# Flamingo-style gated block (selective scan, then a ternary feed-forward): where two one-value loads are issued, products of ones on TensorE in the front, and a new order of the written-out pieces

## The chip, the cores and the metric

One Trainium2 chip, one of its cores. The metric is the device time of one execution in microseconds, the median of three runs. All data is fp32 in HBM at the start and the result goes back there.

## The reference

The input `x` is (4, 256, 256): batch, tokens, channels; the context is (4, 256, 128). Two gated branches are added to `x`, one after the other.

```python
# branch 1: selective scan over the context, gated by silu(layernorm(x))
xi    = einsum('ed,bld->bel', in_proj_w, ctx)              # 256 channels
u     = silu(causal_conv4(xi) + conv_b)
x_dbl = einsum('ke,bel->bkl', x_proj_w, u)                 # 8 dt rows, 16 B rows, 16 C rows
delta = softplus(dt_proj_w @ dt_rows + dt_proj_b)
A     = -exp(A_log)                                        # (256, 16)
state = state * exp(delta*A) + (delta*u) * B_t             # for each of 256 tokens
y_t   = sum_n state[:, n] * C_t[n]
x     = x + tanh(g_xattn) * (y + D*u) * silu(layernorm(x))
# branch 2: per-token 8-bit activations, ternary weights
q     = round(layernorm(x) * 128/absmax)                   # w_gate, w_up: (1024, 256)
h     = silu(gate(q)) * up(q)
x     = x + tanh(g_ffn) * down(act_quant(walsh_hadamard(h)))   # w_down: (256, 1024)
```

The three weight matrices are scaled by the mean of their absolute values and rounded to -1, 0 or 1 inside the kernel.

## The kernel before, in words

The kernel is written by hand, with no scheduler at run time: each engine has a program that is a list of calls of small pieces, in an order written out, and each piece waits on semaphores for what it needs. An engine works through its list strictly in order. The four batches are the outer unit. In the scan the 16 states of a batch are taken two at a time, so there are 32 steps, m = 8 * batch + j. For step m and half h of the channels:

- `decays(m, h)` (ScalarE, L1036) writes exp(delta*A), two activations of 128x255.
- `drive_rows(m, h)` (TensorE, L397) multiplies the transposed delta*u by diagonal matrices of B, so that B*(delta*u) stands in PSUM.
- `scan(m, h)` (DVE, L1611) runs the recurrence over both.
- `C_rows(m)` (TensorE, L444) spreads C over the partitions, `times_C(m)` (DVE, L1694) multiplies, `accumulate(m)` (TensorE, L460) transposes the products into the sum over states.

POOL builds the diagonals (`diagonals(n, i)`, L1432) from the copy of B that `copy_BT(n)` (ScalarE, L1047) makes. It also takes the bf16 pieces of B and C apart (`split`), finishes softplus for later batches, scales weights and does the Walsh-Hadamard stages between 128-wide blocks (`fold_tile`).

The front, before the first scan, makes the first batch's u and delta. Loads come on two queues: SyncE (context, in_proj_w, x_proj_w, context, x, w_gate, w_up, w_down, hadamard; L312 to L323) and ScalarE (identity, conv_w, conv_b, dt_proj_w, the two gates, A_log, dt_proj_b, D; L962 to L973). The first batch's in_proj goes straight from the transposed weights; ScalarE makes the first tap (`first_tap`, L981) and DVE the others (`first_conv`, L1658), then `silu_u(0)` (L1069), `x_dbl(0)` (TensorE, L505), `dt_rows(0)` (L1103), `dt_proj(0)` (L523), `spread(0)` and `softplus(0)` on ScalarE, `first_relu`, `first_rest`, `first_delta` on DVE, `du_T(0)` (TensorE, L430) and `copy_duT(0)` (ScalarE, L1054). Beside it stand the transposes of the tap weights (`setup_in_proj`, L366, copied by `inw_out`) and of the other contexts (`setup_late`, L383, copied by `ctx_out`), which the later batches need, `in_proj(1, h)` (L489), `tanh_gates` (L999, waits for both gates and A_log), `exp_A` (L1004), `first_rstd` (layer norm of x, on ScalarE and DVE) and `weight_abs(m)` (ScalarE, L1023), the sum of absolute values of weight m. `for_silu` and `for_exp` load ScalarE's function table.

The wait that the loads feed is one semaphore for both of the last two:

```python
def spread(n):
    act.wait_ge(pe_draw, n + 1)
    if n == 0:
        act.wait_ge(ld_conv, 16 * 2)      # dtb and dskip
```

`dtb` is wanted by `spread(0)` and `first_relu`, `dskip` by `diag_D` (POOL, L1516) alone.

The tail, after the last scans, is the feed-forward of the last two tiles of tokens of batch 2 and of batch 3, in halves (`last_*`), with `hadamard_mm(2, 1)` (L610), `last_silu` (L1208), `last_fold` on DVE (L1797, L1800), `down(2, 1)` (L632) and `last_hadamard` (L684).

## Time and profile before

| what | value |
|---|---|
| median of 3 runs | 221.41 us (221.14 to 222.14) |
| the profiled execution | 220.58 us, span 218.8 us |
| DVE busy | 188.0 us, 86% |
| PE busy | 188.9 us, 86% |
| ScalarE (ACT) busy | 168.9 us, 77% |
| POOL busy | 108.0 us, 49% |
| mean granted TensorE clock | 0.966 |

The span is from the first to the last instruction; the execution's own time holds 1.78 us beside it. A granted clock of 1.00 is 2.4 GHz, 0.50 is 1.2 GHz. PE's busy time counts the time in flight of pipelined matmuls, so it overstates how full the engine is. In a timeline row, equal instructions that follow each other are merged and counted (x4); an fp32 product stands there as two records, an fp32 transpose as one.

### The profile page before, as it was taken

Reading aid. Unit: us, or ns where it says so; the run is one execution under the profiler, and the core shown is the slowest. Engines: PE = TensorE matmul, PEld = TensorE weight load, DVE = VectorE, ACT = ScalarE, POOL = GpSimd, SP = SyncE. Lnnn points to the kernel's source line nnn. Section 1 sums busy time; section 2 is a strip of 40 time slices with the busy share of each in tenths; the row PEclk is TensorE's granted clock in tenths of the full one; section 3 lists DMA queues with packets and bytes.
Section 4 is the critical chain, followed back from the end, with each engine's and each line's share of the span. In section 5 each row is a group of like instructions: output and inputs, shape, how many; then the busy total and the mean of one; then the engine's idle time right before and its main releaser. Section 6 shows DMA issues by size and latency. Waiting matters only on the chain. (4 is left out here: it accounts for less than half of the span.)

```text
span 218.8 us, 3665 instructions
## 1 busy us (share of the span) xinstructions
PE 188.9 (86%) x1221; PEld 152.7 (70%) x1228; DVE 188.0 (86%) x290; ACT 168.9 (77%) x298; POOL 108.0 (49%) x143
## 2 busy tenths in 40 slices
PE   2747889999899999899999999998998987686773
PEld 1534567887697998578989897797885776653751
DVE  1384938899999999998999999999989996889983
ACT  0278799999989969898967989993997811895373
POOL 1004700678708388029998991299920489510000
PEclk9965599999999999999999999999999999999998
DMA  5894000000000000000000000000000000000001
GB/s 135 264 343 182 0 1 4 0 0 0 3 0 0 3 1 1 0 3 0 1 3 0 0 3 24 1 27 0 0 0 3 25 0 27 0 0 0 27 24 48
DMA packets 8147, 6.33 MB, mean 29 GB/s; under 512 B 2202, under 2 KB 7874, under 8 KB 8130
## 3 DMA queue, kind: packets, MB, share of 16 engines
q1 hardware_dynamic: 6066, 6.01, 8.4%
q10 hardware_dynamic: 2064, 0.10, 0.6%
q8 instruction: 10, 0.16, 0.3%
q14 instruction: 7, 0.06, 0.1%
HBM read 5.05 MB, written 1.05 MB: 28 GB/s over the span
## 5 line engine op out<-in xcount | busy, mean ns | idle before, releaser
L1036 ACT ACTIVATE decay<-delta,zero_c,aneg 128x255 f32<-128x255 f32 x128 | 65.8, 588 | 1.6 <-DVE delta L1686 1.4
L1611 DVE TENSOR_TENSOR_SCAN state<-decay,BC 128x512 f32<-128x512 f32 x32 | 38.8, 1212 | 5.6 <-PE BC L397 3.8
L1611 DVE TENSOR_TENSOR_SCAN state<-decay,UP 128x512 f32<-128x512 f32 x32 | 38.4, 1201 | 1.1 <-issue 0.6
L1694 DVE TENSOR_TENSOR prod<-state,BC 128x1024 f32<-128x1024 f32 x32 | 38.4, 1200 | 0.7 <-PE BC L444 0.5
L1498 POOL TENSOR_TENSOR wnat<-wnat 128x512 f32<-128x512 f32 x18 | 22.9, 1275 | 26.2 <-DVE wnat L1738 25.4
L397 PE MATMUL BC<-diagB,duT 128*128 128x256 f32 x128 | 33.7, 386 | 0.7 <-DVE state L1611 0.5
L460 PE MATMUL PY<-id,prod 128*128 128x128 f32 x256 | 33.2, 273 | 1.1 <-DVE prod L1694 1.1
L397 PE MATMUL UP<-diagB,duT 128*128 128x256 f32 x128 | 33.3, 382 | 0.0
L460 PEld LDWEIGHTS PY<-id,prod 128*128 128x128 f32 x256 | 29.2, 141 | 3.9 <-DVE prod L1694 1.7
L397 PEld LDWEIGHTS BC<-diagB,duT 128*128 128x128 f32 x128 | 22.3, 190 | 5.2 <-issue 2.0
L397 PEld LDWEIGHTS UP<-diagB,duT 128*128 128x128 f32 x128 | 22.7, 190 | 3.6 <-issue 1.2
L1499 POOL TENSOR_TENSOR wnat<-wnat 128x512 f32<-128x512 f32 x18 | 22.9, 1274 | 0.0
L1432 POOL TENSOR_SCALAR_AFFINE_SELECT diagB<-BT 128x1024 f32<-128x1024 f32 x16 | 18.5, 1174 | 6.4 <-PE UP L397 4.4
L1163 ACT COPY hT<-GP 128x1024 f32<-128x1024 f32 x6 | 6.0, 1005 | 13.0 <-PE GP L594 13.0
L444 PE MATMUL BC<-bc,sel 96*128 96x256 bf16 x64 | 12.5, 276 | 1.0 <-DVE prod L1694 1.0
L1454 POOL TENSOR_TENSOR rest<-raw,high 64x256 f32<-64x256 f32 x4 | 2.7, 666 | 21.1 <-ACT raw L1098 21.1
L579 PE MATMUL GP<-wT,qT 128*128 128x512 bf16 x42 | 11.0, 379 | 1.9 <-DVE state L1611 0.9
L444 PEld LDWEIGHTS BC<-bc,sel 96*128 96x128 bf16 x64 | 6.1, 100 | 4.9 <-issue 2.3
L1159 ACT ACTIVATE wq<-GP,zero_c,gs 128x1024 f32<-128x1024 f32 x6 | 7.2, 1206 | 2.6 <-PE GP L579 2.6
L974 ACT ACT_TABLE_LOAD x1 | 1.3, 1283 | 9.4 <-issue 9.4
L579 PEld LDWEIGHTS GP<-wT,qT 128*128 128x128 bf16 x48 | 4.2, 97 | 5.8 <-ACT qT L1174 1.4
L610 PEld LDWEIGHTS GP<-had,hT 128*128 128x128 f32 x64 | 7.7, 192 | 0.8 <-ACT hT L1163 0.6
(250 smaller groups left out, 383.1 us busy)
## 6 DMA issues: line engine op xcount, KB each, us to landing
xs<-in_x_dram SPq DMA_DIRECT2D x1, 1024.0 KB, 8.8
wnat<-in_L_ffn_w_gate_dram SPq DMA_DIRECT2D x1, 1024.0 KB, 12.0
wnat<-in_L_ffn_w_up_dram SPq DMA_DIRECT2D x1, 1024.0 KB, 14.5
wnat<-in_L_ffn_w_down_dram SPq DMA_DIRECT2D x1, 1024.0 KB, 13.9
out_dram<-ot SPq DMA_DIRECT2D x8, 128.0 KB, 1.7
ctxs<-in_ctx_dram SPq DMA_DIRECT2D x1, 384.0 KB, 4.3
ctxs<-in_ctx_dram SPq DMA_DIRECT2D x1, 128.0 KB, 2.9
inw<-n_L_xattn_in_proj_w_dram SPq DMA_DIRECT2D x1, 128.0 KB, 2.6
```

What stands on the lines that cost most here:

```text
L397: last = nc.tensor.matmul(drive_bank(h).rearrange("p (n c l) -> p n c l", n=NB, c=LC)[:, :, c, :], duT[:, b % 2, c, P * h:P * (h + 1)], di ...
L444: last = nc.tensor.matmul(PC[:, L * n:L * (n + 1)], row_pick(DS + NB * j + n), bc3[:, b, :], start=True, stop=True)
L460: last = nc.tensor.matmul(PY[:, E * c + P * h:E * c + P * (h + 1)], prod[:, g % RING, h, n, P * c:P * (c + 1)], id32[:], is_transpose=True ...
L579: last = nc.tensor.matmul(ffn_bank(f, t)[:, 512 * i:512 * (i + 1)], qT[:, h, P * t:P * (t + 1)], w[:, h, 512 * i:512 * (i + 1)], start=(h ...
L610: last = nc.tensor.matmul(dst[:, P * a:P * (a + 1)], hT[:, t, a, :], had[:], start=True, stop=True)
L1036: last = nc.scalar.activation(decay[:, m % RING, h, n, 1:L], delta[:, b % 2, h, 1:L], ACT.Exp, bias=zero_c[:], scale=aneg[:, h, NB * j + n ...
L1159: nc.scalar.activation(sg[:, t], ffn_bank(f, t)[:], ACT.Silu, bias=zero_c[:], scale=gs[:, t:t + 1]).then_inc(act_sg, 1)
L1432: nc.gpsimd.affine_select(diagB[:, i].rearrange("p c n l -> p (c n) l"), BT[:, n % 2, i].rearrange("p c n -> p (c n)").unsqueeze(2).to_bro ...
L1498: nc.gpsimd.tensor_tensor(dst[:, :, 0, :], src[:, :, 0, :], src[:, :, 1, :], ALU.add)
L1499: nc.gpsimd.tensor_tensor(dst[:, :, 1, :], src[:, :, 0, :], src[:, :, 1, :], ALU.subtract).then_inc(done, 1)
L1611: nc.vector.tensor_tensor_scan(state[:, g % STATES, h].rearrange("p n l -> p (n l)"), decay[:, g % RING, h].rearrange("p n l -> p (n l)"), ...
L1694: nc.vector.tensor_tensor(prod[:, g % RING].rearrange("p h n l -> p h (n l)"), state[:, g % STATES].rearrange("p h n l -> p h (n l)"), PC. ...
```

## The change

Three things are changed.

The loads of dtb and dskip leave ScalarE's queue. dtb goes to SyncE's queue between x and w_gate, with a semaphore of its own (`ld_dtb`), dskip to its end behind hadamard (`ld_D`).

TensorE gets pieces that multiply a matrix of ones by itself, into PSUM that is overwritten later; no one reads them. There are 12 calls of `warm` and 5 of `warm_later`, two products each.

The order of the pieces is new in all four programs, over the whole kernel; the pieces themselves are as they were.

```diff
             sp.dma_start(xs[:].rearrange("p b c d -> p (b c) d"), tiles(x)).then_inc(ld_x, 16)
+            with nc.allow_non_contiguous_dma(reason="one value per partition"):
+                sp.dma_start(dtb[:], dt_proj_b.rearrange("(h p) -> p h", p=P)).then_inc(ld_dtb, 16)
...
             sp.dma_start(had[:], hadamard).then_inc(ld_had, 16)
+            with nc.allow_non_contiguous_dma(reason="one value per partition"):
+                sp.dma_start(dskip[:], D.rearrange("(h p) -> p h", p=P)).then_inc(ld_D, 16)
...
+            def warm(i):
+
+                if i == 0:
+                    pe.wait_ge(consts, 1)
+                for n in range(2):
+                    nc.tensor.matmul(X[:, P * n:P * (n + 1)], onesf[:], onesf[:], start=True, stop=True)
+
+            def warm_later(i):
+
+                pe.wait_ge(act_setup, 2)
+                for n in range(2):
+                    nc.tensor.matmul(PB[:, P * n:P * (n + 1)], onesf[:], onesf[:], start=True, stop=True)
...
             setup()
             first_in_proj()
+            warm(0)
             setup_x_dbl()
             setup_dt()
+            warm(1)
+            warm(2)
+            warm_later(0)
+            x_dbl(0)
             setup_in_proj()
             setup_late()
-            x_dbl(0)
+            warm(3)
             dt_proj(0)
+            warm(4)
+            warm(5)
+            C_rows(0)
+            warm_later(1)
+            warm_later(2)
+            warm_later(3)
+            warm(6)
+            warm(7)
+            warm(8)
+            warm(9)
+            warm(10)
+            warm(11)
+            warm_later(4)
             first_B_T()
             in_proj(1, 0)
-            C_rows(0)
             du_T(0)
             in_proj(1, 1)
             drive_rows(0, 0)
             drive_rows(0, 1)
-            gate_T(0)
...
             last_inter_T(1, 0)
             last_inter_T(1, 1)
+            down(2, 1)
             last_hadamard(1, 0)
...
-                with nc.allow_non_contiguous_dma(reason="one value per partition"):
-                    for dst, src in ((dtb, dt_proj_b), (dskip, D)):
-                        act.dma_start(dst[:], src.rearrange("(h p) -> p h", p=P)).then_inc(ld_conv, 16)
                 nc.scalar.preload_act_table_set("silu_and_others")
...
             xpw_out()
+            tanh_gates()
             dtw_out()
-            tanh_gates()
             silu_u(0)
-            inw_out()
-            ctx_out()
             for_exp()
             dt_rows(0)
             high_pieces(0)
+            inw_out()
+            ctx_out()
+            spread(0)
+            softplus(0)
+            exp_A()
+            weight_abs(0)
             first_rstd()
-            spread(0)
-            exp_A()
-            softplus(0)
+            weight_abs(1)
             copy_BT(0)
-            weight_abs(0)
             decays(0, 0)
+            copy_duT(0)
             decays(0, 1)
-            for_silu()
-            copy_duT(0)
-            silu_z(0)
-            silu_u(1)
-            for_exp()
             decays(1, 0)
             decays(1, 1)
+            for_silu()
+            silu_u(1)
+            silu_z(0)
+            for_exp()
...
+            decays(7, 1)
+            decays(8, 0)
+            for_silu()
             conv_out(2)
...
             last_norm(1)
             last_scale(0)
-            quant_down(2, 0)
+            inter_out(2, 1)
             last_tokens_out(0)
             last_scale(1)
+            quant_down(2, 0)
+            for_silu()
             last_silu(0, 0)
...
             first_norm()
-            first_rstd()
             first_relu()
+            first_rest()
             negate_A()
-            first_rest()
             first_delta()
             scan(0, 0)
+            first_rstd()
             scan(0, 1)
```

On POOL `split(0)` now stands ahead of `zero_decays`, and `diag_D` behind `diagonals(0, 2)`. `weight_abs(1)` stood between `decays(5, 0)` and `decays(5, 1)`, and C_rows(31) on TensorE behind `accumulate(30)`; it now stands ahead of `accumulate(29)`.

## Rows read from the trace of the kernel before

**Rows 1.** Granted TensorE clock in 40 slices; then two stretches (clock: third figure from the end).

```profile
PEclk9965599999999999999999999999999999999998
...
12.75:13.00 0.25, 0.05 (x1) 0.00 (x0) 0.25 (x2) 0.00 (x0) 0.00 (x0) 0.60 1.09 365
26.25:26.50 0.25, 0.10 (x1) 0.00 (x0) 0.21 (x2) 0.01 (x1) 0.25 (x1) 0.60 0.00 0
```

**Rows 2.** Busy time by stretch: length; busy of PE, PEld, DVE, ACT, POOL; clock; DMA share, GB/s.

```profile
0.00:31.74 31.74, 19.91 (x70) 14.29 (x71) 15.93 (x50) 18.67 (x37) 7.83 (x24) 0.78 0.52 160
31.74:53.58 21.84, 21.27 (x119) 17.48 (x118) 19.80 (x21) 21.65 (x42) 11.28 (x12) 1.00 0.00 1
53.58:180.84 127.26, 121.69 (x836) 101.79 (x842) 123.05 (x150) 107.23 (x189) 80.43 (x98) 1.00 0.01 4
```

**Rows 3.** The DMA issues: KB each, and us from issue to landing.

```profile
alog<-in_L_xattn_A_log_dram ACTq DMA_DIRECT2D x1, 16.0 KB, 9.2
```

**Rows 4.** Timeline of the front: start, length, engine, line, [idle before, and releaser].

```profile
3.92 0.95 ACTq L970 DMA_DIRECT2D alog<-in_L_xattn_A_log_dram  x1
...
4.25 0.64 PE L343 MATMUL GP<-id,inw 128*128 128x128 f32 x2
...
9.39 1.28 ACT L974 ACT_TABLE_LOAD   x1 [9.39 <-issue]
...
13.23 0.29 ACT L999 ACTIVATE tg<-gates,zero_c 128x2 f32<-128x2 f32 x1 [1.03 <-DMA alog<-in_L_xattn_A_log_dram]
...
14.02 0.91 ACT L1069 ACTIVATE u<-conv,cb 128x256 f32<-128x256 f32 x2 [0.50 <-DVE conv L1658]
...
14.98 2.04 PE L505 MATMUL GP<-u,xpwT 128*104 128x256 f32 x4 [2.18 <-ACT u L1069]
...
18.46 2.07 PE L523 MATMUL GP<-dtlo,dtwT 8*128 8x256 f32 x4 [1.44 <-ACT dtlo L1103]
...
22.95 2.00 ACT L1023 ACTIVATE wq<-wnat,zero_c 128x2048 bf16<-128x2048 f32 x1
...
25.09 1.36 DVE L1686 TENSOR_TENSOR delta<-spl,spa 128x512 f32<-128x512 f32 x1
...
28.00 0.66 PE L430 MATMUL X<-id,du 128*128 128x128 f32 x4 [1.65 <-DVE du L289]
...
28.50 1.88 PE L489 MATMUL GP<-ctxT,inwT 128*128 128x256 f32 x8
...
29.87 0.59 ACT L1054 COPY duT<-X 128x512 f32<-128x512 f32 x1
...
31.74 1.22 DVE L1611 TENSOR_TENSOR_SCAN state<-decay,BC 128x512 f32<-128x512 f32 x1 [3.80 <-PE BC L397]
```

**Rows 5.** Timeline and grouped lines of the same operations at full clock, or with POOL idle.

```profile
L406 PE MATMUL GP<-xpwT,u 128*128 128x16 f32 x8 | 1.0, 252 | 0.0
...
35.16 1.03 PE L505 MATMUL GP<-u,xpwT 128*104 128x256 f32 x4
...
67.99 1.10 PE L523 MATMUL X<-dtlo,dtwT 8*128 8x256 f32 x4
...
190.92 2.05 PE L610 MATMUL BC<-had,hT 128*128 128x128 f32 x16 [1.45 <-ACT hT L1163]
...
199.10 0.69 DVE L1797 TENSOR_TENSOR wnat<-wnat 128x512 f32<-128x512 f32 x1
```

**Rows 6.** Timeline: end of the third weight sum, and two of DVE's waits in the middle.

```profile
51.80 0.19 ACT L1023 ACTIVATION_READ_ACCUMULATOR wq<-wnat,zero_c 128x1 f32 x1
...
64.07 1.22 DVE L1611 TENSOR_TENSOR_SCAN state<-decay,BC 128x512 f32<-128x512 f32 x1 [0.53 <-ACT decay L1036]
...
180.84 1.22 DVE L1694 TENSOR_TENSOR prod<-state,BC 128x1024 f32<-128x1024 f32 x1 [0.27 <-issue]
```

**Rows 7.** Timeline of the tail: the last batch's first silu, and the down product of an earlier one.

```profile
194.19 1.45 ACT L1208 ACTIVATE wq<-GP,zero_c,gs 128x512 f32<-128x512 f32 x2 [0.20 <-PE GP L651]
...
205.29 1.05 PE L632 MATMUL PY<-wT,q2T 128*128 128x256 bf16 x8 [1.10 <-ACT q2T L1179]
```

More of the change, by code:

```diff
@@ L181, in gated_ssm_ffn @@
                              "ld_gate"))
-        ld_cb, ld_conv, ld_w = sem("ld_cb"), sem("ld_conv"), [sem(f"ld_w{i}") for i in range(3)]
+        ld_cb, ld_dtb, ld_D, ld_w = sem("ld_cb"), sem("ld_dtb"), sem("ld_D"), [sem(f"ld_w{i}") for i in range(3)]
         zeroed, consts, decay_zeroed = sem("zeroed"), sem("consts"), sem("decay_zeroed")
@@ L749, in _ @@
             accumulate(0)
+            drive_rows(3, 0)
             C_rows(1)
+            gate_T(0)
             dt_proj(1)
-            drive_rows(3, 0)
             drive_rows(3, 1)
-            in_proj(2, 0)
+            accumulate(1)
             C_rows(2)
@@ L822, in _ @@
             C_rows(14)
+            up(0, 0)
             drive_rows(16, 0)
-            x_dbl(3)
             drive_rows(16, 1)
@@ L827, in _ @@
             accumulate(13)
+            x_dbl(3)
+            drive_rows(17, 0)
+            drive_rows(17, 1)
+            C_rows(16)
+            accumulate(14)
             up(0, 1)
-            drive_rows(17, 0)
-            C_rows(16)
-            drive_rows(17, 1)
-            accumulate(14)
+            drive_rows(18, 0)
             accumulate(15)
-            drive_rows(18, 0)
             drive_rows(18, 1)
             inter_T(0, 0)
-            accumulate(16)
             C_rows(17)
@@ L942, in _ @@
             q2_T(2, 1)
-            down(2, 1)
             last_hadamard(0, 1)
@@ L1271, in _ @@
             decays(4, 0)
+            decays(4, 1)
             softplus(1)
-            decays(4, 1)
+            gate_out(0)
             decays(5, 0)
-            weight_abs(1)
             decays(5, 1)
             weight_abs(2)
-            gate_out(0)
             decays(6, 0)
@@ L1287, in _ @@
             copy_duT(1)
+            for_exp()
+            decays(8, 1)
             dt_rows(2)
[L1289 to L1291 removed]
             copy_BT(2)
+            decays(9, 0)
             high_pieces(2)
[L1294 removed]
             decays(9, 1)
@@ L1334, in _ @@
             decays(20, 0)
+            high_pieces(3)
             decays(20, 1)
+            decays(21, 0)
+            decays(21, 1)
             inter_out(0, 0)
-            decays(21, 0)
             spread(3)
+            softplus(3)
+            quant_down(0, 0)
             rstd2(1)
-            softplus(3)
-            decays(21, 1)
-            quant_down(0, 0)
             decays(22, 0)
@@ L1345, in _ @@
             inter_out(0, 1)
+            decays(23, 0)
+            gate_out(2)
             second_norm(1)
-            gate_out(2)
             q2_out_early(0, 0)
             scale_tokens(1)
-            decays(23, 0)
             decays(23, 1)
             tokens_out_early(1)
-            decays(24, 0)
             quant_down(0, 1)
             for_silu()
-            copy_duT(3)
             silu_gate(1, 0)
             silu_z(3)
+            silu_gate(1, 1)
+            copy_duT(3)
+            for_exp()
+            decays(24, 0)
+            decays(24, 1)
             q2_out_early(0, 1)
-            silu_gate(1, 1)
-            for_exp()
-            decays(24, 1)
             decays(25, 0)
@@ L1534, in _ @@
             diagonals(0, 2)
-            split(1)
+            diag_D()
             diagonals(0, 3)
             diagonals(1, 0)
+            diagonals(1, 1)
+            split(1)
             softplus_tail(1, pool, nc.gpsimd, pool_front_link, 0)
@@ L1562, in _ @@
             fold_tile(0, 1, 2)
-            diagonals(2, 3)
             softplus_tail(3, pool, nc.gpsimd, pool_front_link, 0)
@@ L1579, in _ @@
             second_rstd(2)
+            diagonals(3, 3)
             token_factors(2)
@@ L1960, in _ @@
             times_C(16)
+            gate_times_up(0, 1)
+            scan(18, 0)
             residual(1)
-            scan(18, 0)
             scan(18, 1)
@@ L2016, in _ @@
             times_C(28)
+            scan(30, 0)
             gate_times_up(2, 0)
-            result(1, 0)
-            scan(30, 0)
             scan(30, 1)
             times_C(29)
+            result(1, 0)
             scan(31, 0)
```

272 lines of the change are left out of this document (130 added, 142 removed).

## The prediction, made before the result was known

> **What bounds the kernel now.** First the page's slices and two short stretches beside them (the span is 218.8 us): the TensorE clock is at half in the front only: it fell near 12.8 and came back near 26.4 [rows 1]. Then the busy time of each engine by stretch, cut at three DVE events: the first scan (31.74), the scan that follows the weight means (53.58), and the last product times C (180.84) [rows 2]. The reader should see three regimes. Up to 31.74 no engine is full (DVE 15.93 us busy, ACT 18.67, PE 19.91): a chain of waits. From 31.74 to 53.58 ScalarE is the bound, 21.65 of 21.84 us. From 53.58 to 180.84 DVE is: 123.05 of 127.26, so 4.21 us is all that a better order can win there. After it comes the tail, again a chain.
>
> In the front the timeline gives the chain [rows 4]: table load 9.39, first tap, the DVE taps, u at 14.02, x_dbl at 14.98, dt_proj at 18.46, softplus, delta at 25.09, du, its transposes at 28.00, in_proj(1,1) at 28.50, duT copied at 29.87, drive rows, scan at 31.74.
>
> **Part 1, the loads.** ScalarE issues dtb and dskip before its table load, which starts at 9.39 and takes 1.28. The issues start near 4.9, behind the one of alog [rows 4], so without them the load ends near 6.2 and the first tap can start when PE's in_proj is done, 7.5, instead of 10.69. That is 3.2 us, and DVE's taps end near 10.8 instead of 13.99. But ScalarE's program now has tanh(gates) ahead of u(0), and tanh waits for the load of alog, which landed 9.2 us after its issue at 3.92, at 13.1 [rows 3, 4]; tanh started at 13.23. Tanh (0.29) and dtwT's copy (0.37), overlapping a little, then put u(0) at 13.8. So of 3.2 us only 0.2 arrive: the alog load is late next. (The gap of 0.5 us that u(0) had to DVE's taps goes, and with it the cover of the alog load.) The removed loads were behind alog on their queue. What could hasten it is that dtb's small packets now stand in SyncE's queue where w_gate's large ones stood; bounds 0 and 1.0 us, and I take 0, since every row of its queue landed late and each behind the other. SyncE's weights come one small load later: the first weight sum started at 22.95 with no wait in front of it, behind other work of ScalarE [rows 4], and takes the same place now, so this work hides it; without that cover it would cost one small load, as the rows of alog's queue go 1 to 2 us. dskip goes last; POOL needs it only behind three diagonals. Both cost nothing.
> The Trainium skill ("DMA: Bandwidth & Descriptors", Issuing engines are not separate DMA queues) says that loads issued by ScalarE and SyncE run on the same 16 DMA engines, and another issuer only saves the issue time. By that rule alone alog lands where it did and the sum stays; were it wrong, u(0) would come up to 1.0 us sooner.
>
> **Part 2, the front's new order.** x_dbl(0) now goes ahead of the tap transposes, and the exp table load directly behind u(0). u(0) ends 0.93 after its start: 14.7. x_dbl took 2.04 at half clock and 1.03 at full [rows 4, 5]. PE has a piece of ones just ahead of it, from 13.8, where it had idled 2.2 us. I take the clock, at 1.2 GHz when x_dbl starts, as back at 2.4 GHz before it ends: done about 16.5. But dt_proj(0), which had followed the copy of its rows at once, now stands behind 8 + 6 transposes (0.15 each at full clock: four took 0.66 [rows 4]; 2.1 in all), one warm piece (below, 0.5) and itself costs 1.10 instead of 2.07 [rows 4, 5]: 16.5 + 2.1 + 0.5 + 1.1 = 20.2, against 20.53. Three tenths won. Ends: 19.3 if the clock is full throughout, 22.7 if half throughout (two transposes took 0.64, each 0.42, so 0.21 apart [rows 4]: 16.75 + 3.0 + 0.86 + 2.07).
> Delta and du get faster: POOL's diagonals wait for BT's copy, which now comes after two weight sums. DVE's delta add took 1.36 beside POOL; the same shape took 0.69 with POOL idle [rows 4, 5]. Three such adds give 2.1 us, so du is ready near 25.5 instead of 27.94. This gain finds nobody waiting, for:
>
> **Part 3, the products of ones.** Each piece is two fp32 products of 128 columns, each in two passes: four records. Sixteen such records (the Hadamard of one tile) took 2.05 us at full clock [rows 5]: 0.12 each, 0.47 for a piece; at half clock, by the transposes' 0.21, 0.86 for a piece. Between dt_proj(0) and BT now stand twelve pieces, 5.6 us, and C_rows 0.5. PE does its queue in order, so behind dt_proj(0) come: 5.6 + 0.5, BT 1.0 (the later one at full clock [rows 5]; twice that at half), in_proj(1,0) 1.85, du_T 0.5, in_proj(1,1) 1.85 (1.88 at full clock), and to the start of the scan 1.3 (from 30.38, where the 1.88 of in_proj(1,1) ended, to 31.74) [rows 4]. Sum 12.6. First scan: 20.2 + 12.6 = 32.8, 1.1 later than 31.74. PE reaches du_T about 3.7 us after du is there. In the kernel before PE waited for du 1.65 us; the train takes that cover and more. ScalarE would not have been much sooner: from 20.2 on spread, softplus and exp(A) take 2.6, two weight sums 4.3 (2.0 and a read of 0.19 each [rows 4]), first_rstd 0.6, BT 0.2, decays(0,0) 1.0, together 28.9 for copy_duT against PE's 29.7. So the weight sum in the front costs nothing while the train is there, and takes nearly all its place if it is gone. first_rstd on DVE goes behind scan(0,0): 0.8 us of DVE that had been hidden, in a stretch that ScalarE bounds.
>
> **Part 4, 31.74 to 53.58.** ScalarE set this stretch. From copy_duT(0) at 29.87 to the end of the third weight sum at 51.99 [rows 4, 6] it worked 22.1 us. New work of the same piece list: minus one weight sum 2.2, plus decays(0,1) 1.0 and the silu table load 1.28, which had stood ahead of duT, plus gate_out(0) 0.6: 22.8. It starts at 29.7, so the weight means and scan(6,0) move from 53.58 to about 54.3: +0.7. DVE (19.80 + 0.8 of work) would be ready at 53.4 and is not the bound.
>
> **Part 5, the middle's order.** Two of DVE's waits have their releaser moved: 0.53 at 64.07 for the decays behind a table-load block (decays(8,0) now precede the block) and 0.27 at 180.84 (C_rows(31) now precede two accumulations) [rows 6]. Minus 0.8. The rest of the 4.21 I leave as it is; ends: -3.4 (all but 0.8 goes) and +2.0 (as much again as half of them).
>
> **Part 6, the tail.** ScalarE's silu table load goes behind quant_down(2,0). The token scale no longer waits for it, but silu(0,0), at 194.19 before [rows 7], now comes after quant (1.2) and the load (1.28): near 194.6. Behind two up products DVE's fold starts 0.2 later. down(2,1) (1.05) now stands ahead of last_hadamard(1,0) [rows 7], whose absmax follows directly on DVE: 0.2 to 0.3. Together +0.4, ends 0 and +1.
>
> **Sum.** +0.7 - 0.8 + 0.4 = +0.3 on the profiled execution of 220.58 (218.8 and 1.78 around it). The median of the runs shown is 221.41, 0.83 above that one; the forecast for it is 221.7: no change that can be told.
>
> **Rivals.** One: DVE's waits in the middle close (faster). Place: 53.58 to 180.84, price up to -3.4. For it: the whole middle is reordered and ScalarE gives up a weight sum of 2.2. Against: DVE is 97% busy there. It decides from 2.2 us recovered on (the 0.8 and 1.4 more); with 2.6 the time is 219.9, with 3.4 it is 219.1.
> Two: the new order's waits (slower). A longer block before decays(8,1), C_rows and accumulations later in places; +2.0 gives 224.5 with nothing recovered.
> Three: the clock stays half through the train (slower). Twelve pieces at 0.86 instead of 0.47 are +4.7, BT +0.9, x_dbl to dt_proj +2.5: if all, 229.8. For it: the clock returned only near 26.4 although PE worked from 18.46 with little pause [rows 1, 4]. Against: what ran just before it rose was in_proj(1,0), products over all 128 rows and 256 columns, and the new queue has x_dbl and the ones, of all rows, from 13.8 on.
> Four: the clock never falls. dt_proj(0) ends at 19.3, everything behind it 0.9 sooner: 220.8. It fell near 12.8 although PE had paused only 2.1 us (up to 11.95) and was at work again [rows 1, 4]; the new queue pauses from about 10.3 to 13.8, so I give it little. The Trainium skill ("TensorE: Matmul & The Clock Gate", Why this matters for your kernels) says that a long enough gap between bursts of matmuls drops the clock to half; by that rule this longer pause lets it fall as well, and rival four does not come.
> Five: the loads pay more than I say: alog lands 1.0 sooner, 220.7.
>
> **Numbers.** Forecast, with four and five at its side 0.44 (own range 220.4 to 222.8); one 0.28; two 0.20; three 0.08. A measurement of this kernel can tell 0.5%, 1.1 us. Faster by more (under 220.3): one, and a little of five: 0.30. Slower by more (over 222.5): two, three and the upper edge of the forecast: 0.32. Same: 0.38. Range 218.9 to 224.5.
>
> **What would show it.** First tap near 7.5 but u(0) still near 13.7, tanh waiting for alog. dt_proj(0) ending within 1 us of 20.2. du long done when du_T starts; first scan at 32 to 34. ScalarE full until the third weight sum, near 53. DVE idle between 53.6 and 180.8 about 3.4 us. I am wrong if u(0) comes before 12.8, if the train runs at half clock or costs less than 4 us, or if DVE's idle time in the middle is under 2 or over 5.

## The result, and the profile after

| what | before | after |
|---|---|---|
| median of 20 runs each, same chip | 221.16 us (219.69 to 223.12) | 219.24 us (216.55 to 221.48) |
| ratio, 95% interval | | 0.9887 [0.9854, 0.9919] |
| the profiled execution | 220.58 us, span 218.8 | 220.84 us, span 218.4 |
| mean granted TensorE clock | 0.966 | 0.973 |

The changed kernel is 1.1% faster. Ratios leave out executions more than 1.5% above the fastest of their kernel, here five of after's 20 (with all of them the medians give 0.9913), and in the experiments one of 657.11 us of the kernel before, one of 235.91 us of e6 and up to six of eleven of the kernel before on one chip. I had forecast 221.7 us, no change: 2.5 us too much, with the time inside the range. The profiled execution of after is one of the slower ones of its kernel, so the same kernel's second profile (218.74 us, called e1 below) stands beside it.

The page's clock row and the busy time by stretch, cut at the same three DVE events (columns as in [rows 2]); they answer to [rows 1, 2]:

```profile
PEclk9967999999999999999999999999999999996998
```

```profile
0.00:32.47 32.47, 24.37 (x138) 21.27 (x139) 13.16 (x46) 19.19 (x37) 7.08 (x25) 0.89 0.50 156
32.47:54.66 22.19, 20.86 (x120) 17.29 (x119) 20.52 (x24) 21.74 (x42) 10.16 (x12) 1.00 0.00 1
54.66:180.02 125.36, 121.69 (x837) 101.97 (x836) 122.90 (x149) 107.81 (x188) 80.22 (x98) 1.00 0.01 4
180.02:218.40 38.38, 28.15 (x207) 20.12 (x205) 29.34 (x72) 21.66 (x33) 9.22 (x11) 0.94 0.05 18
```

DVE's busy time in the third stretch hardly moved (123.05 to 122.90), while the stretch lost 1.90 us: its idle time went from 4.21 to 2.46. ScalarE is busy for 21.74 of the 22.19 us of the second stretch, as I had it, but it does not set the length of that stretch (e3 below).

The front of after, from its timeline; these answer to [rows 4]:

```profile
4.75 1.28 ACT L1005 ACT_TABLE_LOAD   x1 [4.75 <-issue]
...
13.12 0.29 ACT L1030 ACTIVATE tg<-gates,zero_c 128x2 f32<-128x2 f32 x1 [4.11 <-DMA alog<-in_L_xattn_A_log_dram]
13.82 0.91 ACT L1100 ACTIVATE u<-conv,cb 128x256 f32<-128x256 f32 x2
...
19.83 1.13 PE L540 MATMUL GP<-dtlo,dtwT 8*128 8x256 f32 x4
...
23.44 2.84 PE L355 MATMUL X<-onesf 128*128 128x128 f32 x24
...
24.72 0.69 DVE L1717 TENSOR_TENSOR delta<-spl,spa 128x512 f32<-128x512 f32 x1
...
29.18 0.60 PE L447 MATMUL X<-id,du 128*128 128x128 f32 x4
29.62 1.88 PE L506 MATMUL GP<-ctxT,inwT 128*128 128x256 f32 x8
29.82 0.58 ACT L1085 COPY duT<-X 128x512 f32<-128x512 f32 x1 [0.70 <-PE X L447]
...
32.47 1.22 DVE L1642 TENSOR_TENSOR_SCAN state<-decay,BC 128x512 f32<-128x512 f32 x1 [6.34 <-ACT decay L1067]
```

Tanh waits 4.11 us for A_log and nothing stands between it and u(0): the wait I had named. DVE's adds have fallen from 1.36 to 0.69, and du_T still comes three microseconds after du. Nearly each time here is what I had written down. The same rows of e1, the same kernel:

```profile
12.17 0.29 ACT L1030 ACTIVATE tg<-gates,zero_c 128x2 f32<-128x2 f32 x1 [3.17 <-DMA alog<-in_L_xattn_A_log_dram]
...
18.43 1.13 PE L540 MATMUL GP<-dtlo,dtwT 8*128 8x256 f32 x4
...
24.03 0.69 DVE L289 TENSOR_TENSOR du<-delta,u 128x512 f32<-128x512 f32 x1
...
27.78 0.60 PE L447 MATMUL X<-id,du 128*128 128x128 f32 x4
...
31.07 1.22 DVE L1642 TENSOR_TENSOR_SCAN state<-decay,BC 128x512 f32<-128x512 f32 x1 [6.35 <-ACT decay L1067]
```

A_log landed 0.95 sooner, the clock came back a little earlier, and all behind it is 1.4 us earlier; from the first scan on the two profiles agree within 0.05 us.

DVE's waits in the third stretch, first of the kernel before, then of after (line, releaser, us in total, times, longest):

```profile
DVE state L1611 <- issue: 0.6, 1, 0.6
DVE state L1611 <- ACT decay L1036: 0.5, 1, 0.5
DVE amax L1721 <- ACT xn L1145: 0.5, 1, 0.5
DVE am L1832 <- PE GP L610: 0.5, 1, 0.5
DVE wnat L1738 <- issue: 0.4, 1, 0.4
DVE state L1611 <- PE UP L397: 0.3, 1, 0.3
DVE q L1732 <- ACT xn L1153: 0.2, 1, 0.2
```

```profile
DVE state L1642 <- issue: 1.7, 3, 0.8
DVE wnat L1769 <- issue: 0.3, 2, 0.2
```

All seven waits of before (2.9 us) are gone, those of feed-forward pieces too. Of the new ones, 0.39 of the 1.7 lies in front of scan(6,0), ahead of the stretch; the rest is 1.6. Which moved piece closed which wait I did not take apart; e6 below shows that the order behind the front does it without the new front.

The tail of after, answering to [rows 7]:

```profile
192.41 1.28 ACT L1263 ACT_TABLE_LOAD   x1
193.71 1.45 ACT L1239 ACTIVATE wq<-GP,zero_c,gs 128x512 f32<-128x512 f32 x2
```

Counted from the last product times C, silu comes at 13.69 instead of 13.35, behind its table load as forecast; e10 below shows that it comes no sooner in the old order.

Where the time went, in us between the DVE events (the last one is the start of the last result's instruction):

| stretch | before | after | e1 | forecast |
|---|---|---|---|---|
| start to first scan | 31.74 | 32.47 | 31.07 | 32.8 |
| to scan(6, 0) | 21.84 | 22.19 | 22.19 | 21.5 |
| to the last product | 127.26 | 125.36 | 125.34 | 126.5 |
| to the last result | 35.32 | 35.68 | 35.66 | 35.7 |

### The profile page after: what moved, and what is told of

Read it like the earlier page. It is cut to its first block, busy times and chain, and to the rows that moved or that the text cites. A ratio compares the mean times of both kernels' runs of the same rounds, so it can differ in the third digit from the quotient of the medians.

```text
span 218.4 us, 3808 instructions
## 1 busy us (share of the span) xinstructions
PE 195.1 (89%) x1296; PEld 160.7 (74%) x1296; DVE 185.9 (85%) x290; ACT 170.4 (78%) x298; POOL 106.7 (49%) x143
## 3 DMA queue, kind: packets, MB, share of 16 engines
HBM read 5.05 MB, written 1.05 MB: 28 GB/s over the span
## 4 chain that ended last, share of the span: by engine, by line
PE 41%; POOL 7%; ACT 6%; DVE 5%; issue 2%; DVEq 0%; POOLq 0%; ACTq 0%
PE PY L477 8%; PE UP L414 7%; PE BC L414 6%; PE GP L596 5%; POOL wnat L1529 3%; POOL wnat L1530 3%; PE GP L627 2%; PE GP L611 2%; PE BC L461 2%; PE UP L649 1%; PE UP L668 1%; ACT ctxs L1200 1%; DVE state L1642 1%; DVE wnat L1828 1%; ACT wq L1239 1%
## 5 line engine op out<-in xcount | busy, mean ns | idle before, releaser
L1529 POOL TENSOR_TENSOR wnat<-wnat 128x512 f32<-128x512 f32 x18 | 22.9, 1273 | 22.4 <-DVE wnat L1769 21.5
L477 PE MATMUL PY<-id,prod 128*128 128x128 f32 x256 | 32.8, 273 | 0.1
L1463 POOL TENSOR_SCALAR_AFFINE_SELECT diagB<-BT 128x1024 f32<-128x1024 f32 x16 | 17.3, 1090 | 22.1 <-ACT BT L1078 15.4
L596 PE MATMUL GP<-wT,qT 128*128 128x512 bf16 x48 | 12.4, 380 | 1.1 <-ACT qT L1205 0.7
L611 PE MATMUL GP<-id,wnat 128*128 128x128 f32 x48 | 6.3, 275 | 2.1 <-ACT ctxs L1200 1.1
L627 PE MATMUL GP<-had,hT 128*128 128x128 f32 x64 | 8.0, 278 | 0.3 <-ACT hT L1194 0.3
```

What stands on the lines that cost most here:

```text
L477: last = nc.tensor.matmul(PY[:, E * c + P * h:E * c + P * (h + 1)], prod[:, g % RING, h, n, P * c:P * (c + 1)], id32[:], is_transpose=True ...
L596: last = nc.tensor.matmul(ffn_bank(f, t)[:, 512 * i:512 * (i + 1)], qT[:, h, P * t:P * (t + 1)], w[:, h, 512 * i:512 * (i + 1)], start=(h ...
L611: last = nc.tensor.transpose(GP[:, P * a:P * (a + 1)], fold[:, t, P * a:P * (a + 1)], id32[:])
L627: last = nc.tensor.matmul(dst[:, P * a:P * (a + 1)], hT[:, t, a, :], had[:], start=True, stop=True)
L1463: nc.gpsimd.affine_select(diagB[:, i].rearrange("p c n l -> p (c n) l"), BT[:, n % 2, i].rearrange("p c n -> p (c n)").unsqueeze(2).to_bro ...
L1529: nc.gpsimd.tensor_tensor(dst[:, :, 0, :], src[:, :, 0, :], src[:, :, 1, :], ALU.add)
```

## The experiments

Every kernel here computes the whole reference. Ratios are to the kernel before on the same chip, with 95% intervals.

**e1: the changed kernel again,** with no edit, for a second look at its front.

> The changed kernel as it is, timed again beside the kernel before. Its first profiled execution had the first scan at 32.47 us (0.73 later than before), the last product times C 0.82 earlier, the end 0.4 earlier, a granted clock of 0.973, yet its runs took between 216.6 and 221.5 us. Theory CLOCK: the runs differ by where the TensorE clock falls to half; an execution that stays at full clock in the front ends 2 to 4 us sooner, and the ones products make that more frequent. Theory ORDER: the gain is the middle's order (DVE waits closed, about 1 to 1.5 us), the same in every execution. CLOCK expects spans between 214.5 and 218.4 that fall as the mean clock rises from 0.973 to 1.0; ORDER expects the gain over the kernel before whatever the clock. Ratio expected 0.989 again.

Measured: 218.74 us (0.9925 [0.9893, 0.9958]). Eleven of its 12 runs lie between 218.5 and 218.9, the kernel before on that chip between 218.6 and 225.6 (35 runs). The third and fourth stretch of the table come out as in after. The front differs, with A_log's landing and the clock.

**e2: no ones; e3: no train** (the ones before dt_proj(0) stay).

```diff
-            warm(0)
...
-            warm(3)
             dt_proj(0)
-            warm(4)
...
             C_rows(0)
-            warm_later(1)
...
-            warm_later(4)
             first_B_T()
```

> The changed kernel without any product of ones (17 pieces, 34 products out), all else the same. CLOCK: the front's clock falls in every execution and comes back late, since in_proj(1,0) follows dt_proj at once; x_dbl and the transposes run at half clock, mean clock 0.95 to 0.97, and the time is 1 to 3 us over that of the changed kernel. ORDER, and my reckoning ahead of the result: PE is free 4.7 us sooner for in_proj(1,0) and du_T, but ScalarE's two weight sums hold BT and duT until 28.9, so the first scan comes at 31.2 to 32 instead of 32.5 and the time falls by 0.5 to 1 us.

> The changed kernel with only the five pieces of ones ahead of dt_proj(0) (warm 0 to 3, warm_later 0); the twelve behind it are out. If the train costs what I said (it puts PE 3.7 us behind du), the first scan comes up to 1.2 us sooner, bounded by ScalarE, and the time falls by up to 1 us. CLOCK: the train keeps the clock up until the drive rows; without it the clock may fall again between 22 and 29 us, where PE has in_proj(1,0) (1.9 us) and waits for du, and the time is the same or 1 us longer.

Measured: e2 220.02 us (0.9966 [0.9929, 1.0002]), e3 219.57 (0.9961 [0.9929, 0.9993]): 1.3 and 0.8 us more than e1 on the same chip (all 12 runs of e3 are above eleven of e1's 12). The train's direct cost is there: du_T starts at 26.81 and 26.93 instead of 27.78. But PE then has nothing to do while ScalarE makes two weight sums ahead of BT's copy, and the clock falls. Timeline of e3 (PE):

```profile
26.93 1.09 PE L447 MATMUL X<-id,du 128*128 128x128 f32 x4 [4.37 <-ACT BT L1066]
...
27.81 3.60 PE L506 MATMUL GP<-ctxT,inwT 128*128 128x256 f32 x8
```

Busy time of e3 in two stretches (columns as in [rows 2]):

```profile
24.00:26.00 2.00, 0.00 (x0) 0.00 (x0) 0.75 (x2) 1.97 (x5) 0.00 (x0) 0.67 0.00 0
26.00:28.00 2.00, 1.07 (x5) 1.10 (x6) 0.00 (x0) 1.78 (x5) 1.14 (x2) 0.50 0.00 0
```

in_proj(1,1) takes 3.60 where after has 1.88, and from du_T to the first scan it is 5.56 us instead of e1's 3.29. In these two profiles the train is worth 1.4 us at the first scan (32.49 against 31.07), in the medians 0.8. My pricing had only its cost.

e3 also tells what sets the second stretch. Its busy time there (columns as in [rows 2]) and one of ScalarE's waits in it:

```profile
32.49:54.68 22.19, 20.86 (x120) 17.28 (x119) 20.50 (x24) 20.09 (x40) 9.50 (x11) 1.00 0.00 1
```

```profile
ACT spr L1134 <- PE GP L540: 1.2, 1, 1.2
```

ScalarE has 1.65 us less to do there than in after and stands still for 1.2 us at one wait alone, for PE's dt_proj(1), and the stretch is 22.19 all the same. In e14 it is busy for 19.66 us, and again the stretch is 22.19. DVE's part is the same in all of them: 20.5 us of work and 1.5 of short waits, none of which the traces put down to ScalarE. In the old order DVE does wait for decays once, 0.6 us, but there too the length does not follow ScalarE's work: e7's ScalarE is busy for 20.52 us, before's for 21.65, and both stretches take 21.8.

**e4: the loads alone,** on the old order.

```diff
+                sp.dma_start(dtb[:], dt_proj_b.rearrange("(h p) -> p h", p=P)).then_inc(ld_dtb, 16)
...
+                sp.dma_start(dskip[:], D.rearrange("(h p) -> p h", p=P)).then_inc(ld_D, 16)
...
-                    for dst, src in ((dtb, dt_proj_b), (dskip, D)):
-                        act.dma_start(dst[:], src.rearrange("(h p) -> p h", p=P)).then_inc(ld_conv, 16)
```

> The kernel before with only the two one-value loads moved to the other queue as in the change. Ahead of the result I gave the move 0.2 us, since tanh waits for the load of A_log anyway, here too: u(0) behind tanh at 13.5 to 13.8 instead of 14.02, same kernel else: time within 0.3 us of before. Rival: the first tap 3 us sooner moves DVE's layer-norm statistics as well and the front gains 1 us or more.

Measured: 222.65 us, 1.0082 [1.0046, 1.0118], slower than before. Timeline of e4, POOL and then PE:

```profile
21.44 1.27 POOL L1517 TENSOR_SCALAR diag<-id,dskip 128x128 f32<-128x128 f32 x2 [19.92 <-DMA dskip<-in_L_xattn_D_dram]
...
25.56 2.04 PE L493 MATMUL GP<-ctxT,inwT 128*128 128x256 f32 x4 [4.97 <-issue]
```

With the old list of POOL `diag_D` stands first, and dskip now comes last: POOL is held up to 21.44, `split(0)` behind it, and in_proj(1,0) waits 4.97 us. So the load's move needs the move of `diag_D`: this is what e7 tests. The profile is of one of the fastest runs (221.05 us) and has its first scan at 32.28, no later than e8's 32.89 below, so it shows the hold but not its price.

**e7: the loads and `diag_D`** behind `diagonals(0, 2)`, on the old order.

```diff
-            diag_D()
             zero_decays()
...
             diagonals(0, 2)
+            diag_D()
```

> The kernel before with the two loads moved, and POOL's diag_D behind diagonals(0,2) as in the change. The loads alone were 0.8 per cent slower, and their trace had TensorE's in_proj(1,0) wait 5 us, until 25.6. My reading: diag_D stood at the head of POOL's list and waits for dskip, which now comes last, so split(0) and with it in_proj(1,0) came late. If so, with diag_D moved in_proj(1,0) starts near 21, the first scan comes near 30.7 to 31 (tanh at 12.1 instead of 13.2), and the time is 0.3 to 1 us below before. Rival: it is the clock, in_proj(1,0) at half; then moving diag_D changes little.

Measured: 219.96 us, 0.9922 [0.9884, 0.9961]. in_proj(1,0) starts at 20.36 and the hold is gone; in time that is 0.9922 against e4's 1.0082. Its one profile (222.10 us, the longest of its 12 runs) does not show where the 0.8% come from: its first scan is at 32.41, with a mean clock of 0.74 up to it, and its third stretch is 128.14.

**e5: only the front of the change; e6: only the rest.**

e5 is the changed kernel with the old lists behind the front's pieces, on all engines; e6 is the kernel before with the new lists there. First some lines of e5 against the changed kernel, then of e6 against the kernel before:

```diff
             accumulate(0)
-            drive_rows(3, 0)
             C_rows(1)
...
-            decays(4, 1)
             softplus(1)
-            gate_out(0)
+            decays(4, 1)
             decays(5, 0)
...
             weight_abs(2)
+            gate_out(0)
             decays(6, 0)
```

```diff
             softplus(1)
+            gate_out(0)
             decays(5, 0)
             weight_abs(1)
             decays(5, 1)
             weight_abs(2)
-            gate_out(0)
             decays(6, 0)
...
             decays(7, 1)
+            decays(8, 0)
             for_silu()
```

> The changed kernel's loads, ones and front (up to the first scan on DVE, the drive rows of step 1 on TensorE, the table load before decays(2,0) on ScalarE, diag_D on POOL), then the old order of the middle and tail; gate_T(0) stands behind C_rows(1), and weight_abs(1) stays in the front. Theory FRONT: the gain of 1 per cent is the front's (A_log's load lands 1 us sooner, and the clock is up from the transposes on): ratio 0.990, first scan near 31.1. Theory MIDDLE: the gain is the DVE waits of the middle; then this kernel is at 0.998 to 1.005 and the next one, with the new middle alone, has the gain.

> The other half: the old loads, no ones, the old front, then the changed kernel's order of the middle and tail; weight_abs(1) stands behind decays(5,0) as it did. FRONT expects no gain, 0.998 to 1.005, with the old spread of some 5 us between executions; MIDDLE expects 0.990 to 0.994. If both halves give something, the sum of the two should be the ratio of the whole.

Measured: e5 222.0 us (1.0007 [0.9971, 1.0044]), e6 220.36 (0.9953 [0.9912, 0.9994]). Each has its part of the gain: e5 the early first scan (31.04), e6 the short middle (125.36). And each loses about 0.8 us in the second stretch, 22.97 and 23.00 instead of 22.19 (the old order has 21.84), where DVE waits for decays. Timeline of e5, then of e6 (DVE):

```profile
42.55 1.22 DVE L1642 TENSOR_TENSOR_SCAN state<-decay,BC 128x512 f32<-128x512 f32 x1 [1.06 <-ACT decay L1067]
```

```profile
51.26 1.22 DVE L1611 TENSOR_TENSOR_SCAN state<-decay,UP 128x512 f32<-128x512 f32 x1 [1.36 <-ACT decay L1036]
```

Here the halves meet: e5 has weight_abs(1) in the front but `gate_out(0)` and `softplus(1)` in their old places, e6 the other way round. That this is the reason I read from the lists; no run moves these pieces alone. The parts do not add: together they give 0.4% where the whole gives 1.1%. In e6's profile the tail takes 36.56 us as well, 0.9 more than in after, since one Hadamard product ran at a granted clock of 0.55 there (3.58 us; 2.05 in after).

**e8: the kernel before again,** with no edit.

> The kernel before, as it is, for a trace from the same chip as the others. Ratio 1.000. The question is the landing of A_log's load: in its first trace tanh started at 13.23. If the landing varies by execution, tanh may start near 12.1 here too and the move of the loads does nothing to it; if the moved loads do it, tanh is at 13.2 again.

Measured: 221.68 us (0.9995 [0.9956, 1.0035]). Tap at 8.71 instead of 10.69, tanh at 13.60, first scan at 32.89; the other stretches as in the first profile (21.82, 127.26, 35.32). Old kernels agree in these and differ in the front.

**e9: the changed kernel with the loads back** on ScalarE's queue.

```diff
                 act.dma_start(alog[:], A_log.rearrange("(h p) n -> p h n", p=P)).then_inc(ld_gate, 16)
+                    act.dma_start(dtb[:], dt_proj_b.rearrange("(h p) -> p h", p=P)).then_inc(ld_dtb, 16)
+                    act.dma_start(dskip[:], D.rearrange("(h p) -> p h", p=P)).then_inc(ld_D, 16)
```

> The changed kernel with dtb and dskip issued by ScalarE again, behind A_log, each still on a semaphore of its own; order and ones as changed. Theory LANDING: the two loads behind A_log on its queue, and their issue ahead of the table load, cost the front about 1 us: tanh starts at 12.7 to 13.6 instead of 12.0 to 12.4, u(0) follows it, the first scan comes 1 us later, time +0.5 to +1.2 us. Rival (my forecast): A_log lands when it lands, whatever stands behind it; then only the table load (near 9.4 again) and the first tap move, u(0) moves by 0.2, and the time is the same.

Measured: 220.20 us, 0.9960 [0.9927, 0.9993]. Its timeline of ScalarE:

```profile
7.97 1.28 ACT L1004 ACT_TABLE_LOAD   x1 [7.97 <-issue]
...
13.28 0.29 ACT L1029 ACTIVATE tg<-gates,zero_c 128x2 f32<-128x2 f32 x1 [2.90 <-DMA alog<-in_L_xattn_A_log_dram]
```

The table load and the tap (9.27) are late again, but tanh still waits 2.90 us for A_log, so they cost nothing. What is left for the loads to cost is the landing, and that these profiles do not settle: tanh starts at 13.28 here, and with the loads moved at 12.17 in e1 but at 13.12 in after. In time, the interval here overlaps those of after and e1 on other chips.

**e10: the old tail** on the changed kernel.

```diff
+            q2_T(2, 0)
             last_tokens_T(1)
...
+            down(2, 1)
             last_hadamard(0, 1)
...
             last_norm(0)
+            for_silu()
...
-            for_silu()
             last_silu(0, 0)
```

> The changed kernel with the old order of the tail (TensorE behind accumulate(31), ScalarE behind inter_out(2,0), DVE from last_residual on). From the last product times C to the last result the new order takes 35.67 us in three traces where the old took 35.32. I expect 35.3 here and a time 0.3 us lower; rival: the tail order is tied to the clock and the difference is not there.

Measured: 219.58 us, 0.9927 [0.9894, 0.9960], and 35.77 us from the last product to the last result: no shorter than after's 35.68. My expectation of 35.3 was missed. The new order's tail is 0.3 us or more longer in every profile, but this does not hang on the order of these pieces. Timeline of before, then of e10 (the transposes ahead of the second Hadamard product, and ScalarE's copy of them):

```profile
188.38 1.09 PE L594 MATMUL GP<-id,wnat 128*128 128x128 f32 x8 [0.24 <-POOL wnat L1499]
...
189.85 1.01 ACT L1163 COPY hT<-GP 128x1024 f32<-128x1024 f32 x1
```

```profile
186.61 1.09 PE L611 MATMUL GP<-id,wnat 128*128 128x128 f32 x8 [1.05 <-POOL wnat L1530]
...
187.74 1.01 ACT L1194 COPY hT<-GP 128x1024 f32<-128x1024 f32 x1 [0.47 <-PE GP L611]
```

Counted from the last product times C, the transposes start at 8.33 instead of 7.54, behind POOL's fold (`fold_tile`), and the copy at 9.46 instead of 9.01: this is the +0.45 of e10. The first silu follows at 13.80 (13.35 in before, 13.69 in after). In after the copy also comes at 9.46. POOL works at its last twelve folds without a pause in e10 and after. My reading, which no run tests by moving the folds alone: with the middle on DVE shorter they end later beside it, and part of the middle's gain comes back as a longer tail.

**e11: tanh behind u(0)** on the changed kernel, one line.

```diff
-            tanh_gates()
             dtw_out()
             silu_u(0)
+            tanh_gates()
```

> The changed kernel with one call moved: tanh_gates behind silu_u(0) on ScalarE, so that the first batch's u no longer waits for the load of A_log. If that wait holds the whole front, as the traces say (tanh idle for 3 us), u(0) starts near 10.8 instead of 12.9, x_dbl and dt_proj follow (exp's table load ends near 13.6), spread(0) is 1.5 to 2 us sooner, and with the train of ones still in front of BT the first scan near 29.3 to 29.8; time -1.3 to -1.8. Rival: ones and transposes at half clock take it back; then less than 0.7.

Measured: 216.04 us, 0.9773 [0.9731, 0.9815]. This was the cover that the loads' gain stood behind. Its timeline:

```profile
7.43 0.84 ACT L1012 ACTIVATE conv<-GP,cw 128x256 f32<-128x256 f32 x2 [1.30 <-PE GP L390]
...
10.77 0.91 ACT L1100 ACTIVATE u<-conv,cb 128x256 f32<-128x256 f32 x2 [1.24 <-DVE conv L1689]
...
12.78 0.30 ACT L1030 ACTIVATE tg<-gates,zero_c 128x2 f32<-128x2 f32 x1 [1.10 <-DMA alog<-in_L_xattn_A_log_dram]
...
14.80 1.13 PE L540 MATMUL GP<-dtlo,dtwT 8*128 8x256 f32 x4
...
28.32 1.22 DVE L1642 TENSOR_TENSOR_SCAN state<-decay,BC 128x512 f32<-128x512 f32 x1 [5.70 <-ACT decay L1067]
```

u(0) now waits for DVE's taps, the last thing that is late, at 10.77 (I had put their end near 10.8). The first scan comes 2.75 us before e1's: u(0) is 2.1 sooner, and x_dbl(0) takes 1.11 us instead of 2.03. The clock reads full throughout in this profile, and these durations agree:

```profile
PEclk9999999999999999999999999999999999999999
```

**e12: a front of its own:** tanh later, BT's transposes ahead of a short train, du_T ahead of in_proj(1, h), all weight sums behind the first scans.

```diff
             dt_proj(0)
+            setup_late()
+            first_B_T()
             warm_later(1)
...
             du_T(0)
+            C_rows(0)
             drive_rows(0, 0)
             drive_rows(0, 1)
+            in_proj(1, 0)
...
             exp_A()
-            weight_abs(0)
-            first_rstd()
-            weight_abs(1)
             copy_BT(0)
```

> A front written anew on the changed kernel: tanh behind u(0), dt_proj(0) ahead of setup_late, six pieces of ones instead of the train, BT and du_T ahead of in_proj(1), its halves between the drive rows; on ScalarE copy_BT and decays(0,0) ahead of the weight sums, the silu block behind decays(3,1), the three weight sums between decays(4,1) and decays(6,0). Reckoned from the traces' rows: first scan near 23 to 24.5 instead of 31; the stretch up to scan(6,0) is then ScalarE's with 4.4 us more work, so scan(6,0) near 50 to 51 instead of 53.3; time -2 to -3.5 us against the changed kernel. Rival: DVE's adds beside POOL's diagonals and a fallen clock take the gain of the front; first scan after 27 and time within 1 us.

Measured: 220.84 us (217.33 to 224.69), 0.9895 [0.9829, 0.9961], slower than e11. The first scan is at 24.74, 3.6 us before e11's, and nothing is left of it at scan(6,0), 51.82 against 50.51. Timeline of e12 (DVE):

```profile
38.75 1.22 DVE L1635 TENSOR_TENSOR_SCAN state<-decay,UP 128x512 f32<-128x512 f32 x1 [1.33 <-PE UP L414]
...
50.80 0.16 DVE L1877 TENSOR_SCALAR wmean<-UP 128x3 f32<-128x3 f32 x1 [2.07 <-PE UP L723]
```

Busy time of e12 from its first scan to scan(6,0):

```profile
24.74:51.82 27.08, 24.07 (x136) 20.55 (x135) 21.07 (x24) 26.89 (x49) 12.21 (x15) 1.00 0.01 2
```

ScalarE works 26.89 of 27.08 us: the weight sums taken out of the front stand here, and an earlier scan does not shorten that list. Here ScalarE does bound the stretch. The profile is of the fastest of its six runs (217.33 us, 1.05 above e11's profiled run); what makes the other five slower, up to 224.69, it does not show.

**e13: e11 with e10's tail,** the two diffs together.

> The changed kernel with tanh_gates behind silu_u(0) and the old order of the tail. e11 had ratio 0.977 and the old tail's stage was 0.3 us shorter in its trace: ratio 0.974 to 0.978, stage from the last product times C to the last result 35.35.

Measured: 216.47 us, 0.9786 [0.9716, 0.9855]; span 214.2, the same as e11's. The two can't be told apart. Its tail takes 35.77 us, as in e10, and not the 35.35 expected.

**e14: e11 without the ones.**

```diff
-            warm(0)
...
-            warm_later(4)
             first_B_T()
```

> e11 without any product of ones. If the ones are worth what they were in the changed kernel (0.4 per cent, by keeping the clock up while TensorE waits for BT), this is 0.8 to 1.5 us over e11 (217 to 217.6) and spreads more. If the shorter wait ahead of x_dbl leaves no pause long enough for the clock to fall, the ones are worth nothing here: within 0.3 us of e11.

Measured: 217.94 us, 0.9855 [0.9782, 0.9927], 1.5 us above e13 on the same chip; first scan at 31.40 instead of 28.19 (its profile is of its slowest run, so the medians are the better price). The same story as e3, from its timeline (PE) and its busy time:

```profile
25.38 1.09 PE L447 MATMUL X<-id,du 128*128 128x128 f32 x4 [4.37 <-ACT BT L1061]
```

```profile
24.00:26.00 2.00, 0.62 (x3) 0.65 (x4) 0.00 (x0) 2.00 (x5) 0.69 (x1) 0.51 0.00 0
```

**e15: the changed kernel on that chip,** with no edit.

> The changed kernel once more, on the chip of the other three: ratio 0.989 to 0.9925, tanh between 12.0 and 12.5, the stages as before (scan(0,0) to scan(6,0) 22.19, to the last product times C 125.35, to the last result 35.67).

Measured: 219.23 us, 0.9899 [0.9826, 0.9971]; first scan 32.59, as in after, although tanh started at 12.68, 0.44 sooner: the clock was at 0.50 up to 18 us and 0.58 from 18 to 20.

**e16: e7 with tanh behind u(0),** the old order otherwise.

```diff
-            tanh_gates()
             silu_u(0)
+            tanh_gates()
```

> The kernel before with the loads moved, diag_D behind diagonals(0,2), and tanh_gates behind silu_u(0); no ones, old order else. e7, the same without the last edit, had tanh at 12.01 and u(0) at 12.21, ratio 0.992. Here u(0) starts near 10.8, 1.4 us sooner. If the wait for A_log is what bounds the front whatever the order, the time falls by about 1.2 us more, ratio 0.986 to 0.988. Rival: dt_proj waits for exp's table load anyway, and what is won is lost in front of dt_rows: ratio 0.990 to 0.993.

Measured: 218.96 us, 0.9900 [0.9812, 0.9987]. u(0) starts at 10.91, but the first scan at 31.11: in the old list tanh, the copies of the transposes and the table load stand between u(0) and dtlo's copy, and dt_proj(0) starts at 16.48 where e11 has 14.80. This is the rival that I had named; against e7 (0.9922) no gain of the moved tanh can be told. On one chip the new order with the moved tanh (e13, 216.47) is 2.5 us better than the old order with it.

## Why the prediction was wrong

**The step that failed: Part 5.** I priced two of DVE's waits in the middle, 0.53 and 0.27, and wrote "the rest of the 4.21 I leave as it is". Measured is -1.9: 125.34 to 125.39 in all twelve profiles with the new order there, 127.25 or 127.26 in all with the old one but e7's. The mechanism is the one I described, DVE's waits; the size was off by 1.1 us. That lies between my term and rival one's point of decision (2.2), nearer to the rival. I had looked up the releasers of two waits, and both went; six others (2.4 us together) stood in the same trace, and for taking them as staying I gave no reason. They all went, and new ones of 1.6 came in their place. DVE's idle time there, which I had put at about 3.4, was 2.46.

**Part 4 had the wrong engine.** I let ScalarE set the stretch from the first scan to scan(6,0) and called DVE "not the bound". Where ScalarE had 1.7 to 2.1 us less to do (e3, e14) the stretch stayed at 22.19. DVE's chain sets it. I had it ready at 53.4 by counting its work alone; it also has 1.5 us of short waits, which I took as nothing, and `first_rstd`, 0.7 us of it, does not hide. The forecast was 21.5 for this stretch, 0.7 too short, and this error hid part of the others. (My own terms there, 29.7 and 22.8 and the 1.6 that follow, give 54.1 for scan(6,0), not 54.3.)

**Part 1's landing** came between my two ends. I took A_log's landing unchanged and put the other end at 1.0 sooner. Tanh, which waits for it, started at 12.67 to 13.60 in four profiles with the loads on ScalarE's queue (mean 13.2) and at 12.01 to 13.12 in fourteen with them moved (mean 12.4). That is 0.8 us at u(0), with ranges that overlap, and after's own 13.12 lies within that of the four. By the rule that I weighed, that another issuer saves only its issue time (the Trainium skill, "DMA: Bandwidth & Descriptors", Issuing engines are not separate DMA queues), A_log lands where it did. The two means speak against this, but no run here settles it, and none shows why a load would land sooner when two small ones behind it are gone.

**Part 2's clock** came back later than I said. I had it back before x_dbl(0) ends; in after it was 0.50 from 14 to 18 us, and the eight transposes of taps took 1.91 in place of 1.2. This is why dt_proj(0) ends at 20.96 and not at 20.2, inside the ends that I gave.

**Part 3 had only one side.** The train is as long as I said: with C_rows (0.4) among it, it runs from 19.49 to 25.33 in e1, at full clock. It keeps PE behind du, by 3.1 us (27.78 less 24.03 and 0.69; I had 3.7). Taking it away brings du_T 0.9 forward. What I left out is that PE without it would stand still for up to 4.37 us behind BT's copy, that the clock falls there, and that in_proj(1,1) then takes twice as long (3.60) and the first drive rows 1.19 to 1.65 us instead of 1.03: 1.4 us lost at the first scan in e3, 0.8 to 1.5 us in the times (e2, e3, e14). The forecast was for the kernel with the train, so this did not shift it. It would have shifted my reading, "takes that cover and more": the train is a gain.

**What came as forecast.** First tap 7.49 (7.5). u(0) 13.82 in after (13.8), with tanh waiting: "the alog load is late next", and e11 shows its worth in the new order, 2.7 us. dt_proj(0) ends at 20.96 in after and 19.56 in e1 (20.2; ends 19.3 and 22.7). First scan 32.47 and 31.07 (32.8). scan(6,0) 54.66 and 53.26 (54.3). Tail +0.35 (+0.4), but by luck: with the old order of the tail it is +0.45 (e10), and what the traces name there is POOL's fold, which I had not priced.

**The sum.** From before to e1 it is -0.67 (front), +0.35, -1.92, +0.34: -1.9 on the span, 218.8 to 216.9. The forecast was +0.3. Of the 2.2 between them the middle is 1.1 and the front 1.7, and the second stretch takes 0.7 back. Most of the front's 1.7 is what e1 has over after, 1.4: A_log 0.95 sooner, and the clock. From before to after's own profile, where A_log landed as I had it, the sum is -0.5, and 0.8 lie between it and the forecast: 1.1 the middle, 0.3 the front, less 0.7 for the second stretch.

**The sign.** I asked for 2.2 us in the middle before the result would be faster. 1.9 were enough where the front paid as well: in e1 the first scan comes 0.67 sooner than in before. In after's own profile it comes 0.73 later, and only 0.4 is left on the span; the medians of 20 runs (1.9 apart) lie with e1. Two gains that I held each for a rival came together, and neither of them needed to reach its limit.

## What to carry to other kernels

Where an order is rewritten, list all the waits of the bounding engine in the stretch and ask of each whether its releaser moved; a wait taken as staying needs a reason as much as one taken as closing. When a small activation that waits for a load stands ahead of the critical one, try moving it behind before hastening the load: one line was worth 2.7 us in the new order (e11), but nothing that can be told in the old one (e16), where other work of ScalarE stood in the same gap. An engine that is busy for 98% of a stretch need not set its length: look whether the others ever wait for it, and whether the stretch gets shorter where it has less to do. Filler on TensorE is priced from both sides, the delay of what stands behind it and what that work costs at half clock when the engine stood still before it (e3).

The best version is e11: 216.04 us, 0.9773 [0.9731, 0.9815]. Against the changed kernel on one chip it is e13 that can be read, with the same front: 216.47 and 219.23 us, 1.3% less.

## What the hardware showed that I had not expected

- Issuing the two one-value loads took ScalarE 2.05 + 2.38 us in the profile of before, 0.81 + 1.58 in e8, 1.20 + 1.86 in e9 and 0.53 + 1.12 in e6, the same instructions in the same place. The 3.2 us that I took for the tap's gain was one execution's; e8 has 1.2.
- The granted clock can read full ahead of its first change where durations say half. In e2 x_dbl(0) took 2.03 us at 14.05, the duration of half clock ([rows 4, 5]: 2.04 and 1.03), and the row of that stretch says 1.00:

```profile
14.00:16.00 2.00, 1.95 (x5) 1.35 (x6) 0.61 (x8) 1.28 (x1) 0.00 (x0) 1.00 1.06 357
```

- The kernel before spread over 7.1 us on one chip (35 runs), the changed one over 1.8 on the same chip (12 runs, eleven of them within 0.4). On the chip of the result it was the other way round, 3.4 and 4.9 in 20 runs each, and on a third the changed kernel spread by 1.8 in six. The front holds what differs between profiles; whether it holds all of the spread stays open.
- Without its loads on ScalarE the old order alone comes to 0.9922 (e7), as far as the whole change, and the one profile of it doesn't show why. That stays open too.
